# Layer 0 of a four-layer sequence kernel: row sums of squares from token-ordered sums, their scales through DRAM

## The chip, the cores and the metric

The kernel runs on one core of one Trainium2 chip. The metric is the device time of one execution in microseconds (us), given as the median of several executions. A profiled execution gives its own time, its span (first to last instruction) and the rows quoted below.

## The reference, cut to what matters

x is (64, 64, 256) in float32, which is 4096 tokens (rows) of D = 256. Four conditioned layers follow each other. The change touches the first one and the normalisation at the head of the second:

```python
def layer0(x, cond, norm_w, up_w, down_w):
    scale = cond @ norm_w.T + 1.0
    ms = jnp.mean(x * x, axis=-1, keepdims=True)
    h = x * (scale[:, None, :] * jax.lax.rsqrt(ms + EPS))
    val, gate = jnp.split(h @ up_w.T, 2, axis=-1)
    h = val * jax.nn.gelu(gate, approximate=False)
    y = act_quant(h) @ weight_quant(down_w).T
    return y + x

def layer1(x, t, ...):
    h = gamma1 * (x * rsqrt(mean(x * x, -1) + EPS)) + beta1   # then q, k, v
    x = x + alpha1 * (softmax(q k / 4) v @ W_o.T)
    h = gamma2 * (x * rsqrt(mean(x * x, -1) + EPS)) + beta2
    return x + alpha2 * ((silu(h @ gate_w.T) * (h @ hidden_w.T)) @ out_w.T)
```

Layer 2 is an adapter whose weights are made from cond, and layer 3 is a conditioned layer norm.

## The kernel before, in words

**Layout.** x stays in SBUF as `x_sb` with the 256 features on partitions (two halves of 128) and the tokens along the free axis. A number that belongs to a token, such as 1/rms, is then needed in every partition, in a row of 4096 columns: that row is `stat`. Layer 0's output y comes out of TensorE the other way round, tokens on partitions.

**Layer 0** goes over 32 tiles of 128 tokens as a software pipeline: one body per tile and engine, written in the order in which each engine executes it, and each helper works on an older tile (its lag). The order is fixed by hand; semaphores hold the engines together. For tile t, step by step:

- POOL `split_tile` makes the scaled input as a high and a low part, TensorE `up_chunk` projects it (24 matmuls of 512 columns per tile, L395), ACT takes the gelu (L503) and DVE multiplies (L620).
- DVE `largest` and `quantise` (L628, L576, L580) make 8-bit values, the SP queue transposes them by DMA (L271), and TensorE `down` multiplies them by the ternary weights (L412, 8 matmuls) into bank 4. It runs at the end of the body of tile t + 2.
- ACT `take_y` scales that to `y` (L494), TensorE `y_transposes` turns it (L431, 2 transposes), and DVE `add_y` adds it to `x_sb` (L569).
- For layer 1's normalisation ACT `square` squares the new x (L486), POOL `sum_squares` adds the two halves (L357), TensorE `row_squares` adds over partitions with a matrix of ones (L420), and DVE `take_row_squares` copies the row to `stat` (L592).

A plain copy of the tokens in token order (`tokens`, a ring of 4, L259) is read from DRAM for the input's own mean square (L478); ACT asks for it two tiles ahead.

**SP** issues, in each body: the transposing DMA, a piece of layer 1's weights (`w_stage`, L262), the tokens of one tile (L259).

**Between layer 0 and 1.** The last three or four tiles of layer 0 are finished inside the first attention tiles: the steps e32 to e36 are calls of layer 0's helpers put between attention's. `early_rstd` on ACT (in the body of tile 28) turns the first 768 columns of `stat` into 1/rms with two loads of activation tables around it (L515 to L520).

**Attention (layer 1)** has 16 tiles of 256 tokens, again one body per tile. ACT `attention_rstd` takes logarithm and exponential of the tile's 256 columns of `stat` (L168, L171). POOL `attention_input` multiplies x by them (L186) and applies gamma and beta (L190, L192) and makes the low part (L195). POOL also divides the softmax (`normalise`, L848) and adds the result to x (`residual`, L857). DVE takes the maxima and subtracts them (L1382, L1385), ACT exponentiates (L1192), DVE sums (L1395, L1399). The body of TensorE is squares (L1033), values (L970), scores (L991), transposes (L1005), output (L1045), keys (L940), weighted values (L1022), scores, transposes, queries (L940), transposes.

The lines that a sentence can't say well: who waits in the middle of the old chain.

```python
def row_squares(pe, s):
    if s.live(5):
        pe.wait_ge(Z["sq_sum_done"], s.at(5) + 1)
        wait(pe, Z["ss_done"], s.at(5))
        pe.wait_ge(Z["x_done"], s.at(3) if s.live(3) else N)
        nc.tensor.matmul(ss_ps, core["ones"][:], sq_sum[:, s.slot(5, 2), :], ...)
```

Of the kernel before, what the change touches and what calls it, by code (L numbers as in the profile page):

```python
# [104 lines left out]
def program(nc, io, out):  # L105
    with ExitStack() as ctx:
        def sb(name, shape, dt=FP32, c=ctx):
# [10 lines left out]
            ident_bf=sb("ident_bf", [P, P], BF16),  # L118
# [5 lines left out]
        with ExitStack() as c0:  # L124
# [10 lines left out]
                            "ln_done rstd_done xn_done h_done h_hi_done h_ready passed".split()}  # L135
        core["softmax"] = [sb(name, [P, 2, 8]) for name in ("mx", "rsum", "rec")]
        core["gen_cond"] = [sb(name, [P, B]) for name in ("gen_cond", "gen_factors")]

        adapter_w = nc.dram_tensor("adapter_w", [B, P * GEN_N], FP32, kind="Internal").ap()
# [24 lines left out]
def attention_rstd(nc, act, core, t):  # L164

    S = core["att_sems"]
    st = core["stat"][:, bass.ds(t * GT1, GT1)]
    nc.scalar.activation(st, st, ACT.Ln, scale=1.0 / D, bias=core["wscale"][:, 3:4]).then_inc(S["ln_done"], 1)  # L168
    act.wait_ge(S["ln_done"], t + 1)
    hold(act, S["passed"])  # L170
    nc.scalar.activation(st, st, ACT.Exp, scale=-0.5).then_inc(S["rstd_done"], 1)  # L171


def attention_input(nc, pool, core, t, k, part):

    x, cond, stat, h, S = core["x"], core["cond"], core["stat"], core["att_in"], core["att_sems"]
    hi, lo = (parts[k] for parts in core["att_parts"])
# [5 lines left out]
    if part == 0:  # L183
        pool.wait_ge(S["rstd_done"], t + 1)
# [20 lines left out]
def layer0(nc, io, core, bank, sb, sem, early):  # L205
# [11 lines left out]
    READY = 3 * GT1  # L217
# [18 lines left out]
    sq, sq_sum = sb("sq0", [P, 2, DH, P]), sb("sq0_sum", [P, 2, P])  # L236
    squared, ss, small, cond_t = sb("squared", [P, D]), sb("ss", [P, N]), sb("small", [P, 4, 4]), sb("cond_t", [C, B])
    y_ps, ss_ps, yt_ps = bank[4][:, 0:D], bank[7][:, 0:P], bank[7][:, P:P + DH * P].rearrange("p (h t) -> p h t", h=DH)
    norm_ps, down_ps, late_ps = bank[7][:, 0:DH * B], bank[7][:, 0:1], bank[7][:, DH * B:4 * DH * B]
    loaded_up, tokens_loaded, stage_loaded = ([sem(f"{n}{i}") for i in range(4)] for n in ("loaded_up", "tokens_loaded", "stage_loaded"))  # L240
    qt_loaded = [sem(f"qt_loaded{i}") for i in range(2)]
    names = ("loaded_norm loaded_cond loaded_vecs loaded_down loaded_x0 loaded_x1 loaded_x norm_ready norm_done cond_ready cond_done "
             "ones_done ident_done up_hi_done up_lo_done down_sum down_total down_step downq_done squared_done mean_done rstd0_done "
             "xs_done xs_hi_done xs_ready up_done gelu_done h_done small_step y_scale_done round_done q_done "
             "y_ready y_done yt_ready x_done sq_done sq_sum_done ss_ready ss_done w1_hi_done w1_lo_done passed sp_passed ve_passed").split()
    Z = {n: sem("z_" + n) for n in names}

    def sync_program(sp):
# [16 lines left out]
        def transpose_q(s):  # L265
            if s.live(3):
                k = s.slot(3, 2)
                sp.wait_ge(Z["q_done"], s.at(3) + 1)
                wait(sp, Z["y_ready"], s.at(5) + 1 if s.live(5) else 0)
                hold(sp, Z["sp_passed"])  # L270
                sp.dma_start_transpose(qt[:, k], q[:, k]).then_inc(qt_loaded[k], 16)  # L271

        def body(s):

            transpose_q(s)
            wait(sp, Z["w1_lo_done"], s.at(3))
            load_stage(s)
            sp.wait_ge(Z["squared_done"], s.at(3))
            load_tokens(s)

# [26 lines left out]
        pipeline(sp, N, 0, 4, body, start=4)  # L307
        for t in range(N, N + 3):
            transpose_q(Step(t, t % 4, N))
# [42 lines left out]
    def sum_squares(pool, s):  # L352
        if s.live(5):
            k = s.slot(5, 2)
            pool.wait_ge(Z["sq_done"], s.at(5) + 1)
            wait(pool, Z["ss_ready"], s.at(6))
            nc.gpsimd.tensor_tensor(sq_sum[:, k], sq[:, k, 0], sq[:, k, 1], ALU.add).then_inc(Z["sq_sum_done"], 1)  # L357

    def gpsimd_program(pool):
        def body(s):  # L360
# [6 lines left out]
            if s.last(-1):  # L367
                attention_input(nc, pool, core, 0, 0, 0)
                attention_input(nc, pool, core, 0, 0, 1)
            if s.last(0):  # L370
                attention_input(nc, pool, core, 0, 0, 2)
                attention_input(nc, pool, core, 1, 1, 0)
                attention_input(nc, pool, core, 1, 1, 1)
            sum_squares(pool, s)
# [3 lines left out]
        pipeline(pool, N, 5, 4, body, stop=N)  # L378
# [36 lines left out]
    def row_squares(pe, s):  # L415
        if s.live(5):
            pe.wait_ge(Z["sq_sum_done"], s.at(5) + 1)
            wait(pe, Z["ss_done"], s.at(5))
# [1358 lines left out]
```

## Time and profile before

| | |
|---|---|
| time, median of 3 runs | 814.53 us (813.87 to 815.04) |
| the profiled execution: its time / its span | 815.97 us / 813.9 us |
| TensorE (PE) busy | 783.1 us, 96% of the span |
| DVE, POOL, ACT busy | 541.9 us, 402.9 us, 375.8 us |
| granted TensorE clock, mean | 0.992 |
| layer 0 up to its last up projection | 0 to 233.3 us |
| attention | to about 425 us |
| the rest of layer 1, layers 2 and 3 | to 813.9 us |

"Busy" of TensorE counts modelled ends of pipelined matmuls, so neighbours overlap: what a group of matmuls costs is the distance to the start of the next one, which the chain of waits gives. An idle time in a timeline row stands in brackets, with what ended it.

### The profile page before, as it was taken

What the parts mean: (1) busy time and instruction counts of PE and PEld (TensorE: products, weight loads), DVE (VectorE), ACT (ScalarE), POOL (GpSimd) and SP (SyncE); (2) the same over time, 40 slices, a digit from 0 to 9 for tenths busy, and PEclk for the clock granted to TensorE, in tenths of its full rate; (3) what the DMA queues carried; (4) which work ended last, traced back from release to release, by engine and by line L of the source; (5) the groups of instructions that cost most, each with busy time, mean ns of one, the idle gap of its engine ahead of it and who ended that gap; (6) DMA issues with size and microseconds to landing.
All of it is one profiled execution on the core that took longest, in us unless ns stands there. A gap on an engine that the chain in (4) does not pass through costs nothing.

```text
span 813.9 us, 19536 instructions
## 1 busy us (share of the span) xinstructions
PE 783.1 (96%) x6860; PEld 630.4 (77%) x6860; DVE 541.9 (67%) x933; ACT 375.8 (46%) x729; POOL 402.9 (50%) x451
## 2 busy tenths in 40 slices
PE   8999999999999899999999999999999999999984
PEld 6788888888888898998988766676767677787772
DVE  4777777777789898898895555555454545444664
ACT  4244444444658688888875324322223222322332
POOL 3655555555596988888883531313131313101565
PEclk9999999999999999999999999999999999999997
DMA  8843333333320100000003087767667676592442
GB/s 248 234 79 78 77 77 77 77 77 78 77 41 7 38 3 1 0 0 0 0 2 104 22 262 234 233 180 223 194 201 205 183 208 193 181 374 98 156 167 104
DMA packets 73731, 97.57 MB, mean 120 GB/s; under 512 B 38608, under 2 KB 48016, under 8 KB 73552
## 3 DMA queue, kind: packets, MB, share of 16 engines
q1 hardware_dynamic: 71088, 92.68, 39.3%
q10 hardware_dynamic: 2592, 4.20, 1.4%
q8 instruction: 34, 0.56, 0.3%
q14 instruction: 17, 0.14, 0.1%
HBM read 67.23 MB, written 21.23 MB: 109 GB/s over the span
## 4 chain that ended last, share of the span: by engine, by line
PE 65%; POOL 16%; issue 8%; DVE 3%; DMA 3%; ACT 3%; SPq 1%; POOLq 1%; ACTq 0%; DVEq 0%
PE bank L1081 21%; PE bank L395 20%; PE bank L1095 11%; PE bank L1115 4%; POOL p_sb L848 4%; PE bank L412 3%; POOL mlp_in L186 2%; DMA early<-in_cond_w 2%; POOL mlp_in L190 2%; POOL x_sb L857 1%; POOL mlp_in L192 1%; POOL x_sb L1665 1%; POOL sums L1659 1%; POOL sums L1654 1%; POOL att_in_lo L195 1%
## 5 line engine op out<-in xcount | busy, mean ns | idle before, releaser
L1447 DVE TENSOR_TENSOR g<-bank,silu 128x512 f32<-128x512 f32 x64 | 44.2, 691 | 106.4 <-ACT silu L1292 56.6
L1292 ACT ACTIVATE silu<-bank 128x512 f32<-128x512 f32 x64 | 38.3, 598 | 111.3 <-PE bank L1081 111.3
L1298 ACT ACTIVATE g_hi<-g 128x512 fp32r<-128x512 f32 x64 | 40.4, 632 | 98.4 <-DVE g L1447 96.4
L395 PE MATMUL bank<-up_hi,xs_hi 128*128 128x512 f32 x256 | 83.0, 405 | 1.6 <-DVE h L620 0.8
L1450 DVE TENSOR_TENSOR g_lo<-g,g_hi 128x512 fp32r<-128x512 f32 x64 | 52.7, 824 | 45.3 <-ACT g_hi L1298 45.3
L395 PE MATMUL bank<-up_lo,xs_hi 128*128 128x512 f32 x256 | 80.6, 397 | 0.7 <-DVE up_lo L657 0.7
L1081 PE MATMUL bank<-mlp_in_hi,w_hi 128*128 128x512 f32 x256 | 80.6, 396 | 0.0
L848 POOL TENSOR_TENSOR p_sb<-p_sb,rec 128x512 f32<-128x512 f32 x64 | 66.7, 1046 | 27.6 <-DVE rec L1399 27.6
L1081 PE MATMUL bank<-mlp_in_lo,w_hi 128*128 128x512 f32 x256 | 79.8, 393 | 0.0
L1081 PE MATMUL bank<-mlp_in_hi,w_lo 128*128 128x512 f32 x256 | 79.7, 392 | 0.0
L395 PE MATMUL bank<-up_hi,xs_lo 128*128 128x512 f32 x256 | 79.4, 392 | 0.0
L620 DVE SCALAR_TENSOR_TENSOR h<-bank,rstd,gelu 128x512 f32<-128x512 f32 x64 | 47.8, 747 | 42.0 <-ACT gelu L503 42.0
L688 POOL TENSOR_TENSOR mlp_in_lo<-mlp_in,mlp_in_hi 128x1024 fp32r<-128x1024 f32 x8 | 22.7, 2836 | 97.9 <-ACT mlp_in_hi L695 97.9
L503 ACT ACTIVATE gelu<-bank,rstd 128x512 f32<-128x512 f32 x64 | 43.9, 687 | 56.2 <-PE bank L395 53.8
L678 POOL TENSOR_TENSOR mlp_in<-x_sb,stat 128x1024 f32<-128x1024 f32 (+1 forms) x8 | 19.1, 2387 | 78.8 <-PE bank L1081 78.6
L395 PEld LDWEIGHTS bank<-up_lo,xs_hi 128*128 128x128 f32 x256 | 48.3, 189 | 12.4 <-DVE up_lo L657 1.9
L395 PEld LDWEIGHTS bank<-up_hi,xs_lo 128*128 128x128 f32 x256 | 48.4, 189 | 11.0
L1081 PEld LDWEIGHTS bank<-mlp_in_lo,w_hi 128*128 128x128 f32 x256 | 48.1, 188 | 11.2
L1081 PEld LDWEIGHTS bank<-mlp_in_hi,w_hi 128*128 128x128 f32 x256 | 47.9, 188 | 11.3 <-issue 0.2
L1081 PEld LDWEIGHTS bank<-mlp_in_hi,w_lo 128*128 128x128 f32 x256 | 48.1, 188 | 11.0
L395 PEld LDWEIGHTS bank<-up_hi,xs_hi 128*128 128x128 f32 x256 | 45.7, 190 | 11.4 <-POOL xs_lo L332 2.0
L1095 PE MATMUL bank<-g_hi,w_hi 128*128 128x512 f32 x128 | 54.2, 423 | 0.0
(193 smaller groups left out, 1916.3 us busy)
## 6 DMA issues: line engine op xcount, KB each, us to landing
gen_hyper<-in_gen_t SPq DMA_DIRECT2D x32, 512.0 KB, 4.9
gen_made<-base_w SPq DMA_DIRECT2D x64, 256.0 KB, 3.9
adapter_w<-gen_made SPq DMA_DIRECT2D x64, 256.0 KB, 3.5
tokens<-in_x_tok SPq DMA_DIRECT2D x32, 128.0 KB, 2.3
w_stage<-in_w_t SPq DMA_DIRECT2D x32, 128.0 KB, 2.4
weight_slot<-adapter_w SPq DMA_DIRECT2D x4, 1024.0 KB, 9.0
w_hi<-adapter_w SPq DMA_DIRECT2D x4, 1024.0 KB, 5.7
w_lo<-adapter_w SPq DMA_DIRECT2D x4, 1024.0 KB, 9.4
```

The source lines that it names most:

```text
L395: last = nc.tensor.matmul(bank[2 * j + part][:, :], (xs_hi, xs_lo)[a][:, k, d, :], up[b][:, d, at:at + 512], start=n == d == 0, stop=n == ...
L412: last = nc.tensor.matmul(y_ps, qt[:, s.slot(2, 2), f, :], downq[:, f, :], start=f == 0, stop=f == FC - 1)
L503: nc.scalar.activation(gelu[:, j, :], bank[2 * j + 1][:, :], ACT.Gelu, scale=rstd0[:, bass.ds(s.at(0), 1)]).then_inc(Z["gelu_done"], 1)
L620: nc.vector.scalar_tensor_tensor(out=h[:, k, j * 512:(j + 1) * 512], in0=bank[2 * j][:, :], scalar=rstd0[:, bass.ds(t, 1)], in1=gelu[:, j, ...
L848: nc.gpsimd.tensor_tensor(pu, pu, rec[:, r % 2, :].unsqueeze(2).to_broadcast([P, 8, L]), ALU.mult).then_inc(A["norm_done"], 1)
L1081: last = nc.tensor.matmul(bank[2 * (f % 2) + i][:, :], w1[a][:, at:at + P], hs[b][k][:, d, :], start=n == d == 0, stop=n == 2 and d == DH - 1)
L1095: last = nc.tensor.matmul(bank[5 + m][:, :], w1[a][:, at:at + P], gs[b][:, f % 2, :], start=f == n == 0, stop=f == FC - 1 and n == 2)
L1115: last = nc.tensor.matmul(ps[B * half:B * (half + 1), :], scaled[rows, :], hyper[rows, k, half, :], start=True, stop=True)
L1292: nc.scalar.activation(silu[:, f % 2, :], bank[2 * (f % 2)][:, :], ACT.Silu).then_inc(S["silu_done"], 1)
L1298: nc.scalar.activation(gs[0][:, f % 2, :], g[:, f % 2, :], ACT.Copy).then_inc(S["g_hi_done"], 1)
L1447: nc.vector.tensor_tensor(g[:, f % 2, :], bank[2 * (f % 2) + 1][:, :], silu[:, f % 2, :], ALU.mult).then_inc(S["g_done"], 1)
L1450: nc.vector.tensor_tensor(gs[1][:, f % 2, :], g[:, f % 2, :], gs[0][:, f % 2, :].bitcast(FP32), ALU.subtract).then_inc(S["g_ready"], 1)
```

## The change

In layer 0, what was in feature order becomes token order:

- A second copy of the tile's tokens (`tokens_again`, a ring of 2) is read from DRAM. DVE `add_tokens` makes y = scale * (down result) + tokens in one operation; `take_y` and `add_y` go.
- TensorE transposes this sum, and ACT `take_x` copies the transposed result over the tile of `x_sb`, where x was.
- ACT `square_rows` squares y with its accumulator, so that a tile's sums of squares lie in one column of `row_squares` (128 x 32). `square`, `sum_squares`, `row_squares` (PE) and `take_row_squares` go.
- For each group of 4 tiles POOL `row_scales` adds EPS and raises to -0.5 (128 x 4). SP stores these 512 numbers to DRAM in token order, and in the next body reads them back, spread over all partitions, into 512 columns of `stat`. `early_rstd` and `attention_rstd` go; `attention_input` waits for the loaded columns instead.
- The bf16 identity, which nothing read, goes.

```diff
+    def add_tokens(ve, s):
+        if s.live(3):
+            t, k = s.at(3), s.slot(3, 2)
+            ve.wait_ge(Z["y_ready"], t + 1)
+            ve.wait_ge(Z["y_scale_done"], t + 1)
+            ve.wait_ge(again_loaded[k], 16 * s.turn(3, 2))
+            wait(ve, Z["yt_ready"], t)
+            wait(ve, Z["rows_done"], t)
+            nc.vector.scalar_tensor_tensor(out=y[:], in0=y_ps, scalar=small[:, s.slot(3, 4), 3:4], in1=again[:, k, :],
+                                           op0=ALU.mult, op1=ALU.add).then_inc(Z["y_done"], 1)
...
+    def square_rows(act, s):
+        if s.live(3):
+            t = s.at(3)
+            act.wait_ge(Z["y_done"], t + 1)
+            wait(act, Z["rows_done"], t)
+            nc.scalar.activation(squared_rows[:], y[:], ACT.Square, scale=D ** -0.5,
+                                 accum_out=row_squares[:, bass.ds(t, 1)]).then_inc(Z["rows_done"], 1)
...
+    def take_x(act, s):
         if s.live(4):
+            act.wait_ge(Z["yt_ready"], s.at(4) + 1)
+            nc.scalar.activation(x[:, :, bass.ds(s.at(4) * P, P)], yt_ps, ACT.Copy).then_inc(Z["x_done"], 1)
...
+    def row_scales(pool, s):
+        if s.slot(0, 4) == 3 and s.live(7):
+            group = bass.ds(s.at(7), 4)
+            pool.wait_ge(Z["rows_done"], s.at(7) + 4)
+            nc.gpsimd.tensor_tensor(row_squares[:, group], row_squares[:, group], wscale[:, 3:4].to_broadcast([P, 4]),
+                                    ALU.add).then_inc(Z["row_mean_done"], 1)
+            pool.wait_ge(Z["row_mean_done"], s.turn(7, 4))
+            nc.gpsimd.tensor_tensor(row_rstd[:, group], row_squares[:, group], wscale[:, 5:6].to_broadcast([P, 4]),
+                                    ALU.pow).then_inc(Z["row_rstd_done"], 1)
...
     # SP, after the transposing DMA, the weights and the tokens of each body:
+        def load_again(s):
+            if s.live(3):
+                wait(sp, Z["y_done"], s.at(4) if s.live(5) else 0)
+                sp.dma_start(again[:, k, :], io["x_tok"][:, bass.ds(s.at(3) * D, D)]).then_inc(again_loaded[k], 16)
+        def store_rows(s):
+            if s.slot(0, 4) == 2 and s.live(10):
+                sp.wait_ge(Z["row_rstd_done"], s.turn(10, 4))
+                sp.dma_start(rstd_row[bass.ds(s.at(10) * P, 4 * P)].rearrange("(t p) -> p t", p=P),
+                             row_rstd[:, bass.ds(s.at(10), 4)], allow_slow_non_contiguous=True).then_inc(Z["row_stored"], 16)
+        def spread_rows(s):
+            if s.slot(0, 4) == 3 and s.live(11):
+                sp.wait_ge(Z["row_stored"], 16 * s.turn(11, 4))
+                wait(sp, stat_loaded, 16 * s.turn(11, 4) - 16)
+                sp.dma_start(stat[:, bass.ds(s.at(11) * P, 4 * P)],
+                             rstd_row[bass.ds(s.at(11) * P, 4 * P)].unsqueeze(0).to_broadcast([P, 4 * P])).then_inc(stat_loaded, 16)
...
     # attention_input, part 0
-        pool.wait_ge(S["rstd_done"], t + 1)
+        pool.wait_ge(core["stat_loaded"], 16 * s.turn(0, 2))
...
     # layer 0's last steps inside attention: DVE
-            first["add_y"](ve, e32)
+            first["add_tokens"](ve, e32)
             ve.wait_ge(A["v_cleared"], 1)
             take_values(a2)
-            first["take_row_squares"](ve, e32)
-            first["add_y"](ve, e33)
+            first["add_tokens"](ve, e33)
             maxima(a2, 0)
             maxima(a2, 1)
-            first["take_row_squares"](ve, e33)
-            first["add_y"](ve, e34)
             sums(a2, 0)
             sums(a2, 1)
+            first["add_tokens"](ve, e34)
             maxima(a2, 2)
             maxima(a2, 3)
```

How the instructions stand now, at the places of which the prediction speaks. First DVE, from the end of layer 0's last body (L628 to L632 before are `largest` of tile 31) to the first softmax maxima. Before:

```order
L592 COPY stat<-bank 128x128
L576 TENSOR_SCALAR h<-h,small 128x1024
L580 TENSOR_SCALAR q<-h 128x1024
L585 TENSOR_SCALAR small<-small,wscale 128x1
L569 TENSOR_TENSOR x_sb<-x_sb,bank 128x2x128
L1411 COPY v_sb<-bank 64x2x8x16
L1412 COPY v_sb<-bank 64x2x8x16
L592 COPY stat<-bank 128x128
L569 TENSOR_TENSOR x_sb<-x_sb,bank 128x2x128
L1382 TENSOR_REDUCE mx<-bank 128x8
```

And with the change (L587 is `add_tokens`, L595 and L599 the quantisation):

```order
L595 TENSOR_SCALAR h<-h,small 128x1024
L599 TENSOR_SCALAR q<-h 128x1024
L604 TENSOR_SCALAR small<-small,wscale 128x1
L587 SCALAR_TENSOR_TENSOR y<-bank,small,tokens_again 128x256
L1404 COPY v_sb<-bank 64x2x8x16
L1405 COPY v_sb<-bank 64x2x8x16
L587 SCALAR_TENSOR_TENSOR y<-bank,small,tokens_again 128x256
L1375 TENSOR_REDUCE mx<-bank 128x8
```

The two copies to `stat` are gone, and what stands behind the quantisation is now the operation whose result TensorE transposes. Further down, the third `add_tokens` (tile 31) stands before the maxima of units 2 and 3:

```order
L1388 TENSOR_REDUCE rsum<-p_sb 128x8
L1392 RECIPROCAL rec<-rsum 128x8
L587 SCALAR_TENSOR_TENSOR y<-bank,small,tokens_again 128x256
L1375 TENSOR_REDUCE mx<-bank 128x8
L1378 TENSOR_TENSOR p_sb<-bank,mx 128x512
```

Before, nothing of layer 0 stood between those sums and maxima (its `add_y` for that tile came two attention steps later).

## Rows read from the trace of the kernel before

**Rows 1.** Busy time by stretch: us, PE, PEld, DVE, ACT, POOL, clock, DMA share, GB/s.

```profile
60.00:220.00 160.00, 160.00 (x848) 134.68 (x847) 118.21 (x234) 70.34 (x168) 85.22 (x162) 1.00 0.34 76
302.90:326.90 24.00, 23.95 (x395) 21.62 (x394) 21.38 (x41) 20.21 (x41) 19.86 (x19) 1.00 0.01 2
```

**Rows 2.** Chain of waits, one tile of layer 0 (start us, us, what).

```profile
151.39 0.22 PE bank L420 x2
151.61 0.22 PE bank L431 x2
151.83 0.87 PE bank L412 x8
152.70 5.49 PE bank L395 x24
```

**Rows 3.** Chain of waits, the up projections of tiles 30 and 31.

```profile
220.78 5.72 PE bank L395 x24
227.82 5.51 PE bank L395 x24
```

**Rows 4.** Timeline of the body of tile 19 (start us, us, engine, what, idle before).

```profile
148.08 0.29 DVE L592 COPY stat<-bank 128x128 f32 x1 [0.18 <-issue]
148.17 0.42 ACT L478 ACTIVATE squared<-tokens 128x256 f32<-128x256 f32 x1 [2.39 <-DMA tokens<-in_x_tok]
148.29 0.41 DVE L569 TENSOR_TENSOR x_sb<-x_sb,bank 128x256 f32 x1
148.94 0.68 ACT L503 ACTIVATE gelu<-bank,rstd 128x512 f32<-128x512 f32 x1
150.16 0.74 DVE L620 SCALAR_TENSOR_TENSOR h<-bank,rstd,gelu 128x512 f32<-128x512 f32 x1
```

**Rows 5.** DMA issues from 60 to 220 us (count, KB, us to landing).

```profile
DMA packets 31334, 12.20 MB, mean 76 GB/s; under 512 B 25444, under 2 KB 31332, under 8 KB 31332
tokens<-in_x_tok SPq DMA_DIRECT2D x23, 128.0 KB, 2.3
qt<-q SPq DMA_TRANSPOSE x24, 3.1
```

**Rows 6.** Timeline of POOL behind the early scales on ACT.

```profile
218.48 0.74 POOL L349 TENSOR_TENSOR w_lo<-w_stage,w_hi 128x256 fp32r<-128x256 f32 x1 [3.75 <-ACT w_hi L509]
```

**Rows 7.** Timelines of PE and DVE between layer 0 and attention.

```profile
234.34 0.49 PE L420 MATMUL bank<-sq_sum,ones 128*128 128x128 f32 x2 [1.02 <-POOL sq_sum L357]
240.56 0.46 PE L420 MATMUL bank<-sq_sum,ones 128*128 128x128 f32 x2 [0.34 <-DVE x_sb L569]
...
248.00 0.66 DVE L1382 TENSOR_REDUCE mx<-bank 128x8 f32<-128x512 f32 x1
...
248.51 1.05 PE L412 MATMUL bank<-downq,qt 128*128 128x256 bf16 x8
...
262.57 0.29 DVE L592 COPY stat<-bank 128x128 f32<-128x128 f32 x1 [0.76 <-PE bank L420]
```

**Rows 8.** Chain of waits, steady attention: what releases POOL's next input.

```profile
350.24 0.42 ACT stat L171
```

**Rows 9.** Timelines of all engines, one attention tile in its steady part.

```profile
337.58 0.49 ACT L168 ACTIVATE stat<-stat,wscale  x1
337.85 0.43 DVE L1411 COPY v_sb<-bank 64x256 f32<-64x256 f32 x1
340.30 0.63 ACT L1192 ACTIVATE p_sb<-p_sb 128x512 f32<-128x512 f32 x1 [0.42 <-DVE p_sb L1385]
343.19 1.04 POOL L848 TENSOR_TENSOR p_sb<-p_sb,rec 128x512 f32<-128x512 f32 x1 [0.53 <-DVE rec L1399]
345.69 0.63 ACT L1263 ACTIVATE sq<-x_sb 128x512 f32 x1 [0.67 <-POOL x_sb L857]
347.87 0.30 PEld L970 LDWEIGHTS bank<-w_hi,att_in_hi 128*128 128x128 f32 x2 [0.22 <-ACT q_sb L1250]
349.81 0.43 DVE L1411 COPY v_sb<-bank 64x256 f32<-64x256 f32 x1
```

More of the change, by code:

```diff
@@ L161, with attention_input @@
 V_OUTB, V_BD, V_BU, V_LNW, V_LNB, V_LINB, V_EVEN, V_ODD = 0, 2, 3, 5, 7, 9, 11, 12
[L164 to L174, printed above, removed]
+def attention_input(nc, pool, core, s, part):
     x, cond, stat, h, S = core["x"], core["cond"], core["stat"], core["att_in"], core["att_sems"]
-    hi, lo = (parts[k] for parts in core["att_parts"])
+    t = s.at(0)
+    hi, lo = (parts[s.slot(0, 2)] for parts in core["att_parts"])
     hb = h[:].rearrange("p h (b l) -> p h b l", b=GB1)
@@ L306, in sync_program @@
                 transpose_q(Step(3, 3, N))
-        pipeline(sp, N, 0, 4, body, start=4)
-        for t in range(N, N + 3):
-            transpose_q(Step(t, t % 4, N))
+                load_again(Step(3, 3, N))
+        pipeline(sp, N, 11, 4, body, start=4, stop=N)
+        for t in range(N, N + 8):
+            s = Step(t, t % 4, N)
+            transpose_q(s)
+            load_again(s)
+            store_rows(s)
+            spread_rows(s)
     def split_tile(pool, s):
@@ L413, in down @@
             last.then_inc(Z["y_ready"], 1)
[L415 to L418, printed above, removed]
-            pe.wait_ge(Z["x_done"], s.at(3) if s.live(3) else N)
-            nc.tensor.matmul(ss_ps, core["ones"][:], sq_sum[:, s.slot(5, 2), :], start=True, stop=True).then_inc(Z["ss_ready"], 1)
     def y_transposes(pe, s):
@@ L634, in body @@
         def body(s):
-            add_y(ve, s)
+            add_tokens(ve, s)
             quantise(ve, s)
@@ L1130, in _ @@
             values(a2)
-            first["row_squares"](pe, e32)
             first["y_transposes"](pe, e32)
@@ L1135, in _ @@
             keys(a2)
-            first["row_squares"](pe, e33)
             first["y_transposes"](pe, e33)
@@ L1142, in _ @@
             transposes(a2, 1)
-            first["row_squares"](pe, e34)
             first["y_transposes"](pe, e34)
@@ L1317, in _ @@
             take_values(a2)
-            first["square"](act, e32)
             nc.scalar.preload_act_table_set("natural_log_exp_and_others")
-            first["take_y"](act, e33)
+            first["take_x"](act, e33)
             act.wait_ge(A["v_ready"], 1)
@@ L1324, in _ @@
             exponentials(a2, 1)
-            first["square"](act, e33)
+            first["square_rows"](act, e33)
             take_keys(a2)
@@ L1328, in _ @@
             take_queries(a2)
-            first["take_y"](act, e34)
+            first["take_x"](act, e34)
             exponentials(a2, 3)
-            first["square"](act, e34)
+            first["square_rows"](act, e34)
             take_transposed(a2, 0)
```

151 lines of the change are left out of this document (52 added, 99 removed).

## The prediction, made before the changed kernel ran

> **What bounds the kernel now.** I read the busy time by stretch first. In layer 0's loop TensorE is busy for all of 160 us, the clock at its full level (1.00, that is 2.4 GHz), while DVE has 118 us, POOL 85 and ACT 70 [rows 1]. So a tile costs what TensorE executes in it. The chain of waits says what that is: 0.22 us for `row_squares` (L420), 0.22 for the transposes, 0.87 for `down`, 5.49 for the up projections, together 6.80 us, one piece directly behind the other [rows 2]. In a steady attention tile TensorE is nearly full too (23.95 of 24.00 us for two tiles), but DVE, ACT and POOL have 21.4, 20.2 and 19.9 us, and 12 us per tile may just as well be the length of a circle through all of them [rows 1]. Between the two stages TensorE stands still several times [rows 7]. After attention nothing is changed.
>
> **The sum is made against the profiled execution (815.97 us)**, which is 1.44 us above the median shown.
>
> **1. Layer 0's loop on TensorE.** `row_squares` runs in the bodies of tiles 5 to 31. In 26 of them (5 to 30) it lies before the last up projection, each 0.22 us on the bounding engine [rows 2]: 26 x 0.22 = **-5.7 us**. Nothing is added on TensorE. Whether the other engines keep up with 6.58 us per tile is the question of the next points.
>
> **2. DVE in the loop.** Before: L592 (starts 148.08) and L569 (148.29, 0.41 us) stand in front of the quantisation [rows 4]. Now it is one `add_tokens`, also one PSUM operand and one SBUF operand of 256 columns, so I take L569's 0.41 us; the 0.21 us of L592 go. It waits for more than `add_y` did, for `down`. But `down` of the tile ends at 145.9 (151.83 + 0.87 = 152.70 is the same point one body later, minus 6.80 [rows 2]), and DVE only gets there at 148.1 [rows 4]: 2.2 us in hand. Cost 0.
>
> **3. ACT in the loop.** One copy replaces another, and the square is now taken with an accumulator, as L478 is. L478, its reading and `take_y` together take 0.77 us (148.17 to 148.94 [rows 4]), so the square becomes at most 0.36 us longer, between the two gelus, where ACT has idle time: the gelu of the first half starts at 148.94, and its product (L620) is over at 150.90, 1.8 us before TensorE needs the bank at 152.70 [rows 2, 4]. What ACT waits for is its token load, 2.39 us in this body [rows 4]. Cost 0, the cover is this 1.8 us.
>
> **4. POOL.** 0.5 us of `sum_squares` per tile goes from an engine with half its time free; two tiny operations per four tiles come. Cost 0 in the loop.
>
> **5. The DMAs.** `tokens_again` is one more load like `tokens` (2.3 us to landing [rows 5]), about 8 us of bodies before DVE wants it: it is requested behind the quantised tile's transposing DMA two bodies earlier, so there is more than one body (6.6 us) against 2.3 us. The queues move 76 GB/s at a share of 0.34 [rows 1]; this adds 128 KB per 6.6 us, 20 GB/s. The store of 512 numbers of 4 bytes has no equal in the trace. Lower bound: nothing, it is issued behind all that the body needs, and 4 us of quiet follow until the next transposing DMA. Upper bound, by the nearest row: a transposing DMA is 25,444 / 24 = 1,060 packets below 512 B and lands after 3.1 us [rows 5], so 512 pieces should take less than that. I take 0. The read back is asked for a body later and each group is needed long before, except the last one, for attention tile 14. SP's own waits (for y two tiles back, for POOL's scale, for the store) are all over when it gets to them. The Trainium skill, "DMA: Bandwidth & Descriptors" (Specifications; Rules for kernel authors), speaks against this store: a non-contiguous last dimension becomes one descriptor per element, and below 512 B the engine does a read-modify-write. [...]
>
> **6. The early scales on ACT.** Two table loads, a logarithm and an exponential go. They held POOL for 3.75 us [rows 6], and one body later TensorE shows a hole: the chain has 5.72 us instead of 5.49 in the body of tile 30 [rows 3]. **-0.23 us.** No other hole is to be seen there.
>
> **7. Between the layers.** Call E the end of the last up projection, 227.82 + 5.51 = 233.33 [rows 3]. Behind it TensorE waited 1.02 us for `sum_squares`. This stop goes, but the time isn't won: the next stop (0.34 us, ended by DVE's L569 at 240.5) hangs on DVE, which from E on does product, maximum, quantisation, scale, addition. Now the transposes of tile 29 wait for `add_tokens` at the same place of that row, so this stop grows by what the first one loses. What really leaves is L592 ahead (0.21) and L420 itself (0.22): **0.4 us** ahead of before. Then comes a new wait: `add_tokens` of tile 31 stands before the maxima of units 2 and 3 and needs `down` of tile 31. Before, these maxima started at 248.00, ahead of that `down` (248.51, 0.87 us long) [rows 7]. Now they start behind `down` and an addition: 248.51 + 0.87 + 0.41 - 0.4 = 249.4 + about 0.1 for the semaphores, 1.3 to 1.5 us late, and with them exponentials 2 and 3 and all queued behind them. Against this stand, in the next body, three L592 and one L569 that leave DVE, L420 twice, and the stop of 0.76 us in front of the last L592 [rows 7], together some 2.1 us on DVE's row. Net I take **-0.5 us** for the stage. Bounds: the delay stays whole and only 0.5 us comes back, +0.9; or nothing is late and all comes back, -2.1.
>
> **8. Steady attention.** `attention_rstd` goes: two operations of 0.49 us and less per tile on ACT. The chain of waits passes through it in every second tile [rows 8], which would promise up to 0.9 us per pass. I count 0, because the circle that has to close every 12 us doesn't contain it: DVE's copy of the values at 337.85, maxima, sums, then POOL's division (343.19, which had waited 0.53 for DVE), the addition to x, ACT's square (345.69, had waited 0.67 for POOL), the queries, TensorE's weight load (347.87, had waited 0.22 for ACT's queries), DVE's next copy at 349.81, 11.96 us later [rows 9]. L168 (337.58) lies where ACT afterwards waits 0.42 us for DVE anyway [rows 9]. It just waits longer.
>
> Sum: -5.7 - 0.23 - 0.5 = **-6.4 us**: 809.6 for the profiled execution, **808.1** for the median.
>
> **The rivals.**
> - **A, attention gets faster.** If ACT's part closes the circle after all, each of about 11 steady tiles wins up to the 0.22 us by which TensorE waits for ACT's queries [rows 9]: -2.4 us more, 805.7. For it: the chain goes through L171 [rows 8]; against it: the 0.42 us of slack behind it. 0.15.
> - **B, the new order is paid in full.** DVE's wait for the last `down` is handed on into the POOL-heavy tiles and isn't made good: +0.9 instead of -0.5, 809.5. 0.15.
> - **C, slower: the store clogs the queues.** If 512 pieces keep the DMA engines so long that the next tile's tokens come late, ACT holds both gelus, and TensorE stops in 7 of the 32 bodies. From where: tokens are issued 0.9 us before the store and again 6.6 us later; they may land 2 us later than now before L620 misses TensorE. So it begins when a store takes more than about 5.7 + 2 = 7.7 us, and to undo 6.4 us and lose the 1.6 us that could be measured, each must cost 8/7 = 1.1 us more: 8.8 us per store. At 10 us the loss is 16 us less 6.4, 824.1. The 3.1 us for twice the number of pieces [rows 5] speaks against it; 4-byte writes to DRAM are what no row shows. 0.05.
> - **D, it is not the ones-matmul that filled the gap**: the transposes, now directly behind an up projection, take over its weight-load time and only half of the 0.22 us is won, 2.9 us less: 811.0. The rows show no idle time between pieces, so I give it 0.05.
>
> **The numbers.** The forecast (808.1, its own range 807 to 809) has 0.6. The range, 804.5 to 811, takes in A, B and D and the bounds of point 7, and leaves out C. A measurement of this kernel can tell about 0.2%, 1.6 us, from no change; A, B, D and the forecast are all faster by more. Faster 0.92, same 0.03, slower 0.05.
>
> **What would show it.** Right: the chain's up projections in layer 0 follow each other at 6.58 us; the body of tile 30 has no hole; behind E one stop of about 1.5 us in front of the transposes of tile 29, ended by `add_tokens`; a wait of about 1.5 to 2 us in front of the third `add_tokens`; attention tiles still 12.0 us apart, with ACT's wait for DVE in front of the exponentials grown by nearly 1 us. Wrong: TensorE idle in every fourth body (C), transposes or `down` longer in the chain (D), attention tiles 11.8 us apart (A), or a waiting `add_tokens` in the loop itself, which would refute point 2.

## The result, and the profile after

**835.34 us** median (832.72 to 836.58, 4 runs) against 814.78 for the kernel before beside it (813.87 to 816.31): ratio **1.0246**, 95% interval 1.0217 to 1.0276. The change makes the kernel 2.5% slower; the forecast was 808.1 us. The profiled execution took 834.95 us, with a span of 833.2.

I cut each profile at two marks: the last start of a matmul of the group `up_hi,xs_hi`, shortly before layer 0's up projections end (L395 before, L429 after), and the start of the first MLP matmul (L1081, L1079). All in us; the first column is from the program's start.

| kernel | layer 0's last | first MLP | span | between the marks | from MLP to the end |
|---|---|---|---|---|---|
| before | 232.0 | 428.3 | 813.9 | 196.3 | 385.6 |
| the change | 236.2 | 441.5 | 833.2 | 205.3 | 391.7 |

So 19.3 us of span came in three places: 4.2 in layer 0, where 5.9 should have been won; 9.0 between the marks; 6.1 behind them, where nothing was changed.

Busy time by stretch of the changed kernel (us, PE, PEld, DVE, ACT, POOL, clock, DMA share, GB/s), to be read beside [rows 1]:

```profile
60.00:220.00 160.00, 151.34 (x773) 123.29 (x772) 114.75 (x204) 63.90 (x182) 91.10 (x151) 1.00 0.47 103
302.90:326.90 24.00, 23.89 (x400) 21.59 (x396) 21.43 (x41) 18.65 (x36) 19.90 (x18) 1.00 0.01 2
260.00:300.00 40.00, 33.06 (x518) 30.18 (x517) 26.77 (x51) 23.40 (x45) 28.76 (x27) 0.87 0.13 29
785.00:833.00 48.00, 31.42 (x510) 24.56 (x506) 24.93 (x44) 14.28 (x26) 28.06 (x29) 0.81 0.34 122
```

TensorE, busy all the time in layer 0 before, now stands still for 8.7 of 160 us. Steady attention is what it was. Behind layer 0 and at the end the granted clock is down.

**Layer 0.** The chain of waits through one of the stops:

```profile
164.26 1.25 SPq L267
165.70 0.43 SPq L257
166.23 5.97 DMA tokens<-in_x_tok
172.45 0.07 ACT squared L502
173.39 0.70 ACT gelu L528
174.21 0.76 DVE h L632
175.01 1.19 PE bank L429 x4
```

The tokens take 5.97 us instead of 2.3 [rows 5], ACT holds its gelus for them, and TensorE waits for the bank. The chain has such a wait at 108.94, 137.73, 166.23, 195.20 and 223.65, in every fourth body. What SP had issued ahead (its timeline):

```profile
160.52 0.41 SPq L281 DMA_DIRECT2D rstd_row<-row_rstd  x1
166.23 0.39 SPq L254 DMA_DIRECT2D tokens<-in_x_tok  x1
170.64 0.35 SPq L290 DMA_DIRECT2D stat<-rstd_row  x1
```

L281 is the store of 512 numbers, L290 waits until it is complete: 10.1 us. The waits on SP's queue add them up (queue, line, released by: us, times, longest), and the DMA page shows how little the engines do:

```profile
SPq L102 <- DMA rstd_row<-row_rstd: 35.3, 8, 9.7
```

```profile
DMA packets 38009, 16.41 MB, mean 103 GB/s; under 512 B 28534, under 2 KB 37366, under 8 KB 38006
tokens<-in_x_tok SPq DMA_DIRECT2D x23, 128.0 KB, 2.7
rstd_row<-row_rstd SPq DMA_DIRECT2D x6, 2.0 KB
```

Share 0.47, median of the tokens still 2.7: a mean hides a stop that comes in one body of four.

**Between the layers.** Timeline and chain of waits:

```profile
244.30 0.44 PE L456 MATMUL bank<-ident,y 128*128 128x128 f32 x2 [1.41 <-DVE y L587]
253.10 0.48 DVE L587 SCALAR_TENSOR_TENSOR y<-bank,small,tokens_again 128x256 f32<-128x256 f32 x1 [2.04 <-PE bank L446]
...
270.73 0.69 DVE L1375 TENSOR_REDUCE mx<-bank 128x8 f32<-128x512 f32 x1 [6.98 <-remote]
270.83 0.60 ACT L1196 ACTIVATE pt_sb<-bank 128x512 f32<-128x512 f32 x1 [4.14 <-remote]
```

```profile
263.58 7.17 another core or an unknown queue
```

The first two rows are the two waits that the forecast named. The other three are new: DVE and ACT stand still together and go on at 270.7. SP goes on at 270.87, released by the last store (issued at 260.63). The profile names no releaser ("remote"), but the semaphores are the program's own. DVE waits for the one that TensorE's scores count up, ACT for the one of TensorE's transposes:

```profile
263.03 1.10 PE L993 MATMUL bank<-k_sb,q_sb 32*64 32x128 f32 x32
268.97 0.27 PE L1007 MATMUL bank<-ident,p_sb 128*128 128x128 f32 x1 [0.50 <-issue]
```

The scores end at 264.13 by the profile, and the trace records their two signals at 270.70 and 270.75; the transposes' first is recorded at 270.80. Meanwhile TensorE goes on starting matmuls, until 268.97. So what comes 6.6 us late is TensorE's signals. (Some other semaphore records of this stretch are missing in the trace, so of the other engines it says less.) Two queues that bring instructions move one transfer each in that stretch, at 263.1 and 266.6. TensorE stands from 269.24 to 273.34 and has a clock of 0.60 in the 10 us from 270 on.

**The ending.** A wait of TensorE that the kernel before has nowhere in its ending (line, released by: us, times, longest):

```profile
PE bank L1591 <- issue: 3.1, 1, 3.1
```

From 791.9 on TensorE stops in the middle of a row of matmuls, waiting for nothing that the profile shows; the clock is 0.50 to 0.54 in the 6 us from 794 on.

### The profile page after: what moved, and what is told of

The parts are those of the page before. It is cut to its first block, busy times and chain, and to the rows that moved or that the text cites. A ratio compares the mean times of both kernels' runs of the same rounds, so it can differ in the third digit from the quotient of the medians.

```text
span 833.2 us, 19402 instructions
## 1 busy us (share of the span) xinstructions
PE 782.3 (94%) x6796; PEld 626.7 (75%) x6796; DVE 540.5 (65%) x900; ACT 360.6 (43%) x731; POOL 408.7 (49%) x435
## 4 chain that ended last, share of the span: by engine, by line
PE 53%; POOL 15%; issue 10%; DMA 8%; DVE 7%; SPq 3%; ACT 2%; another core or an unknown queue 1%; POOLq 1%; DVEq 0%; ACTq 0%
PE bank L1079 20%; PE bank L1093 11%; PE bank L429 10%; DMA tokens<-in_x_tok 4%; POOL p_sb L855 4%; PE bank L1113 4%; POOL mlp_in L179 2%; POOL mlp_in L183 2%; DMA early<-in_cond_w 1%; POOL mlp_in L185 1%; PE bank L1602 1%; POOL x_sb L864 1%; PE bank L1614 1%; DVE h L632 1%; PE bank L446 1%
## 5 line engine op out<-in xcount | busy, mean ns | idle before, releaser
L429 PE MATMUL bank<-up_hi,xs_hi 128*128 128x512 f32 x256 | 82.2, 402 | 3.3 <-POOL xs_lo L360 1.6
L1079 PE MATMUL bank<-mlp_in_hi,w_hi 128*128 128x512 f32 x256 | 80.6, 396 | 0.0
L1079 PE MATMUL bank<-mlp_in_lo,w_hi 128*128 128x512 f32 x256 | 79.8, 393 | 0.0
L632 DVE SCALAR_TENSOR_TENSOR h<-bank,rstd,gelu 128x512 f32<-128x512 f32 x64 | 47.9, 748 | 49.1 <-ACT gelu L528 48.5
L1079 PE MATMUL bank<-mlp_in_hi,w_lo 128*128 128x512 f32 x256 | 79.7, 392 | 0.0
L429 PE MATMUL bank<-up_lo,xs_hi 128*128 128x512 f32 x256 | 79.4, 391 | 0.0
L429 PE MATMUL bank<-up_hi,xs_lo 128*128 128x512 f32 x256 | 79.1, 390 | 0.0
L1375 DVE TENSOR_REDUCE mx<-bank 128x8 f32<-128x512 f32 x64 | 43.9, 686 | 19.4 <-PE bank L993 11.9
L1079 PEld LDWEIGHTS bank<-mlp_in_lo,w_hi 128*128 128x128 f32 x256 | 48.1, 188 | 11.2
L1079 PEld LDWEIGHTS bank<-mlp_in_hi,w_hi 128*128 128x128 f32 x256 | 47.9, 188 | 11.3 <-issue 0.2
L1079 PEld LDWEIGHTS bank<-mlp_in_hi,w_lo 128*128 128x128 f32 x256 | 48.1, 188 | 11.1
L429 PEld LDWEIGHTS bank<-up_lo,xs_hi 128*128 128x128 f32 x256 | 47.9, 188 | 11.1 <-DVE up_lo L665 0.9
L429 PEld LDWEIGHTS bank<-up_hi,xs_hi 128*128 128x128 f32 x256 | 45.5, 188 | 14.0 <-DVE h L632 2.7
L429 PEld LDWEIGHTS bank<-up_hi,xs_lo 128*128 128x128 f32 x256 | 48.1, 188 | 10.4
## 6 DMA issues: line engine op xcount, KB each, us to landing
weight_slot<-adapter_w SPq DMA_DIRECT2D x4, 1024.0 KB, 10.1
```

The costliest lines, as they stand in the source:

```text
L429: last = nc.tensor.matmul(bank[2 * j + part][:, :], (xs_hi, xs_lo)[a][:, k, d, :], up[b][:, d, at:at + 512], start=n == d == 0, stop=n == ...
L632: nc.vector.scalar_tensor_tensor(out=h[:, k, j * 512:(j + 1) * 512], in0=bank[2 * j][:, :], scalar=rstd0[:, bass.ds(t, 1)], in1=gelu[:, j, ...
L1079: last = nc.tensor.matmul(bank[2 * (f % 2) + i][:, :], w1[a][:, at:at + P], hs[b][k][:, d, :], start=n == d == 0, stop=n == 2 and d == DH - 1)
L1375: nc.vector.tensor_reduce(mx[:, r % 2, :], sc, AX.X, ALU.max).then_inc(A["max_done"], 1)
```

## The experiments

Theory T: a store in 4-byte pieces takes 8 to 10 us until it is signalled, and whatever is issued behind it, tokens, weights, instructions, is signalled only after it. R1: it is the second token copy. R2: any small store to DRAM costs this. T's part on instructions was my reading of the stop behind layer 0; no run shows it, and experiment 5 speaks against it.

**1. Wider pieces.**

```
-  rstd_row[...].rearrange("(t p) -> p t", p=P)    # 512 pieces of 4 bytes
+  rstd_row[...].rearrange("(p t) -> p t", p=P)    # 128 pieces of 16 bytes
   (attention_input reads stat[:, group].rearrange("p (q f) -> p f q", f=4))
```

> The same 2 KB per store, but written as 128 pieces of 16 bytes instead of 512 of 4, and POOL reads the scales in the order in which they then stand; everything else, the second copy of the tokens included, as in the change. Theory T (a store of 512 pieces takes 9.7 us until its completion is signalled, and every DMA issued behind it, tokens, weights, the program's own instructions, is signalled only after it): with a quarter of the pieces, between a token load's 2.4 us and 9.7 us, about 2.4 + 7.3/4 = 4.2 us per store, below the 7.7 us at which TensorE begins to feel it; layer 0 ends near 227 us, the 7 us stop near 264 us is gone, in all 806 to 811 us. Rival R1 (it is the second token copy, its load or the longer row of SP's waits): stays at 833 to 837 us. Rival R2 (any store of this kind to DRAM costs the 9.7 us, whatever its pieces): stays there too, with the store still at 9 to 10 us.

813.31 us (809.44 to 816.05), ratio to before 0.9991 (0.9975 to 1.0008). The store takes 1.6 us (247.6 to 249.2, where SP waits for nothing else), no stop in layer 0, none between the marks. R1 and R2 fall: the second copy is still there, and so is a store of 2 KB. The median is 2 us above the expectation; the profiled execution (809.44) has a clock of 0.994, the slowest (816.05) 0.984.

**2. The scales turned on TensorE.**

```
+  nc.tensor.transpose(bank[5][0:4, 0:P], row_rstd[:, 0:4], ident)
+  nc.scalar.activation(row_t, bank[5][0:4, 0:P], ACT.Copy)
-  store of row_rstd[:, 4 columns] as 512 pieces of 4 bytes
+  store of row_t as 4 pieces of 512 bytes, two bodies later
```

> The four columns of scales are turned by one small transpose on TensorE per four tiles, ACT copies the result, and the store is 4 pieces of 512 bytes; it is issued two bodies later. Theory T: the store takes about as long as a token load, 2 to 3 us, no stop in layer 0 and none near 264 us: 807 to 811 us, against 814.8 before and 835.3 for the change. R1: stays near 835 us. R2: store still 9 to 10 us, time near 835 us.

809.47 us (808.08 to 811.01), ratio **0.9936** (0.9919 to 0.9954). Its window and its last store with the read back behind it:

```profile
60.00:220.00 160.00, 160.00 (x836) 133.02 (x836) 122.54 (x218) 70.22 (x201) 99.21 (x160) 1.00 0.45 109
```

```profile
256.91 0.29 SPq L282 DMA_DIRECT2D rstd_row<-row_t  x1
258.25 0.36 SPq L291 DMA_DIRECT2D stat<-rstd_row  x1
```

Store 1.3 us, TensorE full again. This is the change without its fault, and it wins most of what was forecast.

**3. The stores alone, in the kernel before.**

```
+  eight stores of 512 x 4 bytes from a constant tile, at the change's places in SP's row
```

> The kernel before, unchanged, plus the eight stores of 512 numbers of 4 bytes at the same places of SP's row as in the change, from a tile that is set once; nobody waits for them and nothing reads them, so the output is unchanged. No second token copy, no read back. Theory T: every fourth body loses 2 to 2.6 us, some 8 to 10 us in layer 0, where before loses nothing, and a stop of several us comes soon after layer 0 when instructions are fetched behind the last store: 826 to 834 us. R1: 814 to 816 us, as before. R2: as T.

819.49 us, ratio 1.0058 (1.004 to 1.0077): slower as T says, by 5 us and not by 12 to 19. The tokens behind a store take 4.75 to 6.00 us here too. Four bodies take 28.05 us (120.16 to 232.36 over 16) against 27.23: 0.8 us per store, where the change loses 2.2 (28.56, from 117.53 to 231.76 over 16, against 26.39 in x2_turned). Part of it is seen: the next tokens are issued 6.3 us behind the store here (162.43, 168.73) and 5.7 in the change, and the bodies are 0.22 us longer. The rest I can't account for. And there is no stop behind layer 0 (196.9 us between the marks), against the forecast. The last store goes out at 246.8, hardly earlier than the one that brings a stop in experiment 10 (247.41), and an instruction transfer follows it at 248.6; why it holds nothing up stays open.

**4. Only the last two stores wider.**

```
+  rows = rows.rearrange("(p t) -> p t", p=P) if after the loop else rows.rearrange("(t p) -> p t", p=P)
```

> The change with only its last two stores (those after the loop) written as 128 pieces of 16 bytes; the scales of tiles 24 to 31 come out in another order of tokens, nothing else is changed. It separates layer 0 from what follows. Theory T: layer 0 ends at 237.5 us as in the change (at 235 to 237.5, since the last but one store lies near its end), the stop of 7.2 us near 264 us is gone together with most of the low clock behind it: 9 us off, 824 to 828 us, and down to 820 us if the low clock at the end of the program was a consequence. If the stop near 264 us has nothing to do with the last store: 833 to 837 us.

831.26 us (829.89 to 832.85): 4 us off, not 9. Between the marks 197.6 us: the 7.2 us stop is gone, as T says, and the clock is 1.00 from 270 us on (0.83 in the 10 us before). But layer 0 ended at 242.4 instead of 236.2, with a clock below 1 in several places, and the ending stayed at 391.1 us: no consequence of that stop alone.

**5. The stores by themselves**, on SP while it is idle in attention.

```
+  for each shape: sp.dma_start(shape).then_inc(s, 16); sp.wait_ge(s, ...)
```

> The stores by themselves: the kernel before, in which SP, idle during attention, issues one DMA after another and waits for each. The output is unchanged, nothing reads what they store. In this order: stores of 512, 256, 128 and 1024 pieces of 4 bytes; stores of 128 pieces of 16, 8 and 32 bytes; a load of 128 KB like the tokens'; the 512-piece store with such a load right behind it; the 128 pieces of 16 bytes with a load right behind; a load with the 512-piece store right behind it; last a read of 512 pieces of 4 bytes. Theory T: 9.7 us for 512 pieces, 1.6 us for 128 pieces of 16 bytes, about 2.3 us for the load alone, but over 9 us for the load that stands behind the 512 pieces, near 2.5 us for the one behind the 16-byte pieces, and 2.3 us for the load that stands in front. If the price is per piece: about 5.5, 3.5 and 18 us for 256, 128 and 1024 pieces. If it is the 4-byte width and not the number: 128 pieces of 4 bytes near 9 us as well. Rival to T: the load behind the store takes 2.3 us too, then the stops in layer 0 have another cause.

Timeline of SP; a DMA's time is the distance to the next row, since SP waits in between (not between rows 0.4 us apart, issued as a pair). In order: 512, 256, 128, 1024 pieces of 4 bytes (L823); 128 of 16, 8, 32 bytes (L827); a load; 4-byte store and load; 16-byte store and load.

```profile
279.94 0.39 SPq L823 DMA_DIRECT2D lab_row<-rstd  x1
288.15 0.37 SPq L823 DMA_DIRECT2D lab_row<-rstd  x1
297.41 0.33 SPq L823 DMA_DIRECT2D lab_row<-rstd  x1
305.04 0.36 SPq L823 DMA_DIRECT2D lab_row<-rstd  x1
315.84 0.33 SPq L827 DMA_DIRECT2D lab_row<-rstd  x1
318.29 0.33 SPq L827 DMA_DIRECT2D lab_row<-rstd  x1
321.10 0.32 SPq L827 DMA_DIRECT2D lab_row<-rstd  x1
322.50 0.33 SPq L830 DMA_DIRECT2D lab_in<-in_x_tok  x1
324.62 0.37 SPq L823 DMA_DIRECT2D lab_row<-rstd  x1
325.03 0.51 SPq L830 DMA_DIRECT2D lab_in<-in_x_tok  x1
333.20 0.32 SPq L827 DMA_DIRECT2D lab_row<-rstd  x1
```

512 pieces 8.2 us, 256 9.3, **128 still 7.6**, 1024 10.8; 16, 8, 32 bytes wide 2.4, 2.8, 1.4. The load: 2.1 alone, **8.2 behind the 4-byte store**, 4.7 behind the 16-byte one (333.56 to 338.24, more than I expected). The busy share of the DMA engines, 40 slices of the first store's 8.2 us:

```profile
DMA  0000370000000000000000020000000000000000
```

The pieces are moved in slices 5 and 6, about 1.2 us after the issue; then 7 us of silence until the signal (the 2 is an instruction transfer). So a busy share can't show this cost.

The run itself took 831.81 us (one execution; the kernel before beside it 813.28). Two stops like the change's lie in its attention:

```profile
309.77 5.44 another core or an unknown queue
326.97 6.56 another core or an unknown queue
```

The first ends at 315.2, about when the store of 1024 pieces is signalled (SP goes on at 315.84), the second at 333.5, as the 512 pieces with the load are (333.20). Again TensorE's score signals are what comes late, by 4.7 and 5.8 us; and in the second stop no queue moves instructions (none from 316 to 340 us; the whole run has 34 and 17 transfers on the two queues, as before has, so none is missing). So a held fetch of instructions isn't what this stop waits for. The other four 4-byte stores of the run bring no stop, so one more condition is missing.

**6. The widths.**

```
+  store(lab_row[0:16].rearrange("(p t) -> p t", t=1), 16, 1)    # 16 pieces of 4 bytes; the others alike
```

> Again the kernel before with DMAs one at a time on the idle SP during attention: stores of 1, 16 and 128 pieces of 4 bytes, of 128 pieces of 8 and of 12 bytes, of 512 pieces of 8 bytes; reads of 128 pieces of 4, 8 and 16 bytes; a store of 128 pieces of 8 bytes with a load of 128 KB behind it; the store of 128 pieces of 4 bytes with a load behind it; a load; a read of 512 pieces of 4 bytes; a load. If it is the width of 4 bytes that costs, whatever the number: 7 to 9 us for 128 pieces of 4 bytes, probably for 16 too, and 2.5 to 3.5 us for 512 pieces of 8 bytes and 12-byte pieces. If the number matters as well: under 4 us for 1 and 16 pieces, over 4 us for 512 of 8 bytes. Reads: 2 to 3 us all, if only the write to DRAM is slow; 7 to 9 us for 4-byte reads, if the width alone decides. The load behind 4-byte pieces 7 to 9 us, behind 8-byte pieces below 5.

Read in the same way: 1, 16, 128 pieces of 4 bytes 1.1, 3.0, 7.6 us; 128 of 8 bytes 4.5, of 12 bytes 3.5; **512 of 8 bytes 3.25**. Reads of 128 pieces of 4, 8, 16 bytes 3.7, 1.7, 2.5, and of 512 scattered 4-byte pieces 2.1. A load behind the 8-byte store 5.1, behind 128 4-byte pieces 7.9 (with a stop of 4.3 us in attention). Each is one measurement, and 128 pieces of 8 bytes took 2.8 us in experiment 5, so differences of 2 us say little. Neither simple rule holds: for 4-byte pieces written to DRAM the number counts up to about 128 and hardly beyond, and 512 pieces of 8 bytes are no dearer than 128. The run took 818.03 us (one execution, before beside it 816.22).

**7. The store on ACT's queue.**

```
-  sp.dma_start(rstd_row[...], row_rstd[...])
+  nc.scalar.dma_start(rstd_row[...], row_rstd[...])    # behind square_tokens, every fourth body
```

> The change with its store of 512 pieces of 4 bytes issued by ACT, on its own DMA queue, at about the same time as before by SP; the read back is asked for one body later. Theory T in the form that one queue works in order: tokens on SP's queue land in 2.4 us again, layer 0 ends near 227 us, the stop near 264 us is gone unless instructions share that queue: 808 to 813 us, plus up to 1 us for the eight issues on ACT. Theory T in the form that the 16 engines signal in order whatever the queue: tokens still land after 5 to 6 us in every fourth body, 831 to 837 us.

855.75 us, ratio 1.0514 (1.0477 to 1.0552), worse than the change and above both forecasts. A stop (timelines of SP and ACT):

```profile
174.40 0.39 ACTq L516 DMA_DIRECT2D rstd_row<-row_rstd  x1
178.46 0.38 SPq L254 DMA_DIRECT2D tokens<-in_x_tok  x1
186.00 0.35 SPq L282 DMA_DIRECT2D stat<-rstd_row  x1
186.84 0.42 ACT L492 ACTIVATE squared<-tokens 128x256 f32<-128x256 f32 x1 [8.48 <-DMA tokens<-in_x_tok]
```

The store is on another queue, and the tokens on SP's still wait for it: the hold passes across queues. Here the store takes up to 11.6 us and the tokens are asked for 4 us behind it, hence the longer stops. The Trainium skill, "DMA: Bandwidth & Descriptors" (Queues, rings and completion order), says that a semaphore's increment lands only after every earlier write of the same DMA engine, across its queues. Experiments 5 and 7 agree; by that rule the forecast would have had to put the store's full time in front of the next tokens.

**8. A stop without stores**, in the kernel before.

```
+  SP: ten loads of 128 KB, one behind the other; PE waits for the last before attention's loop
```

> The kernel before with nothing of the change: TensorE alone is held at the start of attention's loop until ten small loads, one behind another, have landed, a stop of some 8 to 14 us from about 252 us on, of the kind that the change has at 264 us. If a stop of that length lets TensorE's granted clock fall behind it and moves the rest of the program so that its ending meets a low clock too, the time grows by the stop plus 4 to 8 us, and the mean clock of the runs is 0.975 to 0.985 as in the change. If a stop costs its own length only: the time grows by just that, with a clock of 0.992.

831.37 us (827.16 to 833.37), ratio 1.0209; clocks 0.980 to 0.984. TensorE stood from 249.0 to 261.0, and its clock was 0.50 from 256 to 270. From the MLP to the end it took 387.7 us, with such a wait in its ending:

```profile
PE bank L1613 <- issue: 2.6, 1, 2.6
```

At the first MLP matmul this profile is 13.7 us behind before, at its end 15.8: the ending costs 2.1 us more without any store in the program (the medians, of other executions, differ by 18.1). But a late arrival alone doesn't do it. Experiment 5's profile reaches the MLP at 444.1, 15.8 us late, and takes 385.7 us from there with no such wait; x1_pieces16 reaches it early, at 420.9, and has one of 2.0 us. All six profiles of the change and of the versions that don't turn the scales have a wait of 1.8 to 3.4 us there, the four of the turned version none; of the variants of the kernel before, this one and x10_widths (2.3 us) have it, x3_before_store and x5_alone don't. So it goes with the program rather than with the time of arrival.

**9. The third addition behind the maxima.**

```
-  add_tokens(e34); maxima(a2, 2); maxima(a2, 3)
+  maxima(a2, 2); maxima(a2, 3); add_tokens(e34)
```

> The version with the turned store, and the third addition of tokens between the layers put behind the maxima of units 2 and 3 instead of ahead of them. If that new wait is what makes the stretch from layer 0's end to the MLP's first tile 1.5 us longer than before (196.5 us against 195.0): 1 to 2 us faster than the turned version, 807.5 to 808.5 us. If the stretch is bound otherwise (transposes that wait for ACT's copies of x, or the additions themselves): no change, 809 to 810 us, or slower, since the last transposes of layer 0 come later.

808.53 us, ratio 0.9944 (0.9921 to 0.9967), by the runs no better than the turned version. By the traces the stretch between the marks goes from 197.8 to 195.6 us. Ahead the turned version, then this one:

```profile
241.05 0.48 DVE L609 SCALAR_TENSOR_TENSOR y<-bank,small,tokens_again 128x256 f32<-128x256 f32 x1 [2.05 <-PE bank L449]
244.43 0.41 PE L459 MATMUL bank<-ident,y 128*128 128x128 f32 x2 [2.54 <-ACT x_sb L531]
```

```profile
241.13 0.48 DVE L609 SCALAR_TENSOR_TENSOR y<-bank,small,tokens_again 128x256 f32<-128x256 f32 x1
241.67 0.44 PE L459 MATMUL bank<-ident,y 128*128 128x128 f32 x2 [0.16 <-DVE y L609]
```

The addition waits 2.05 us for `down`; the maxima, ACT's exponentials and ACT's copy of x queue behind it, and the transposes wait 2.54 us for that copy. I ran both again side by side, with the 16-byte version in the same order:

> The version with the turned store once more, beside the two that follow on the same chip. 808 to 811 us.

> The same with the third addition behind the maxima, once more beside it. In the two profiles TensorE's first MLP matmul came 2.2 us sooner after layer 0's last one; if that is a property of the order, this version is 1 to 2 us faster than the turned one here too; if it is eaten by the ending, the two are within 1 us.

> The version with 128 pieces of 16 bytes, which needs neither the small transpose nor ACT's copy, with the third addition behind the maxima: layer 0 as there, the stretch between the layers 1 to 2 us shorter, 807 to 812 us, where the spread is the ending's: x1_pieces16 ran from 809.4 us at a clock of 0.994 to 816.1 at 0.984.

811.67 (ratio 0.9946), **809.09 (0.9919, 0.9898 to 0.994)** and 812.32 us (0.9945). Now the order is worth 2.6 us in the medians and 2.2 between the marks (197.7 and 195.5), though the intervals overlap. The 16-byte version stays 3 us behind, its clock at 0.986 to 0.992; its profile has a wait of 1.8 us in the ending, and 390.8 us from the MLP to the end. The best version beats the kernel before by 0.6 to 0.8%.

**10. All but the last two stores wider.**

```
+  rows = rows.rearrange("(t p) -> p t", p=P) if after the loop else rows.rearrange("(p t) -> p t", p=P)
```

> The reverse of x4_last_two: the first six stores are 128 pieces of 16 bytes, only the two after the loop keep their 512 pieces of 4 bytes; the scales of tiles 0 to 23 come out in another order of tokens, nothing else is changed. Theory T: layer 0 ends at 225 to 227 us as in x1_pieces16 (the seventh store is issued near its end), the last store still holds the next fetch of instructions: a stop of 5 to 7 us soon after it with a low clock behind, the stretch from layer 0's last matmul to the MLP's first 7 to 9 us longer than the 197.9 us of x1_pieces16, and the ending, which comes some 8 us later than there, with or without its own stop: 818 to 826 us. If the stop near 264 us came from the delays of layer 0 and not from the last store: that stretch stays at 198 us, 810 to 815 us.

819.2 us, ratio 1.005 (1.003 to 1.007). Layer 0 is whole (last matmul at 223.1), the last store (4-byte) is issued at 247.41, and:

```profile
251.88 5.48 another core or an unknown queue
```

```profile
257.03 0.34 SPq L293 DMA_DIRECT2D stat<-rstd_row  x1
```

The stop ends at 257.36, as the store is signalled; from 250 to 258 us the DMA page has two packets, both of them instructions. Between the marks 203.7 us against x1_pieces16's 197.9, behind them 389.6 against 386.7, with a stop of 3.13 us in the ending (776.67). DVE waits for TensorE's score signals here too (recorded 4.9 us late). So the last store costs 5.8 us by itself. The ending is dearer too, but x1_pieces16 has a stop of 2.0 us in its own, so that isn't shown to be the store's doing.

## Why the prediction was wrong

**Points 1 and 6, right.** From the first steady up projection to the last (28 bodies) before takes 190.75 us (37.07 to 227.82), x2_turned 184.84 (34.98 to 219.82): -5.91, forecast -5.93. D did not happen, and the covers of points 2 to 4 held: TensorE full for 160 us. Not priced: in that version the first steady body starts 2.1 us sooner. About half of it is the profile of before, whose clock is 0.83 from 20 to 30 us (x3_before_store, with all of its work, starts there at 36.02); the rest I did not trace.

**Point 5, the step that failed.** "Upper bound, by the nearest row: a transposing DMA is ... 1,060 packets below 512 B and lands after 3.1 us". That row was near in the number of pieces and far in their kind: it writes to SBUF, and the price lies in 4-byte writes to DRAM, 7.6 us for as few as 128. The range ended at 3.1 us although no row showed such a write, as rival C says itself. "SP's own waits (...) are all over when it gets to them" fell with it (35.3 us of waits for the stores). The store's term in the sum was 0. It measured 2.2 us per store in layer 0, 12.2 us at layer 0's last up projections (236.2 against x2_turned's 224.0), and 7.5 us more between the marks.

**Rival C, right in its mechanism.** It put the threshold at 7.7 us, hence 2.4 us per store of 10.1; measured 2.2. It had no term for the last store, behind which TensorE's signals come late: 5.8 us alone (experiment 10) and 7.5 in the change (205.3 against x2_turned's 197.8), nor for the ending (391.7 against 386.2). So its 824.1 fell 11 us short, and 0.05 was far too little for the only case whose price had no row.

**Point 7, wrong beyond its bounds.** -0.5 forecast, +0.9 the upper bound, +1.5 measured (196.3 to 197.8 in x2_turned). The new wait was named and was real (2.04 us at DVE); I let the work that leaves DVE pay for it and did not follow it on to ACT's copy of x and the transposes (2.54 us). With the order turned round the stretch is 0.7 us shorter than before (195.6).

**Point 8, right.** DVE's copy of the values comes at 339.00 and 351.04:

```profile
339.00 0.43 DVE L1404 COPY v_sb<-bank 64x256 f32<-64x256 f32 x1
351.04 0.43 DVE L1404 COPY v_sb<-bank 64x256 f32<-64x256 f32 x1
```

12.04 us, with ACT's two operations gone. A is false.

**Open:** why x3_before_store loses only 0.8 us per store; why TensorE's signals come late beside some of the 4-byte stores and not beside others; and what makes the ending dearer. In the four profiles with a stop of about 3 us there (the change, x4_last_two, x11_all_but_two, x7_other_queue) the part behind the MLP takes 389.6 to 391.7 us; in the others it takes 384.7 to 387.8, except x9c_pieces16_maxima with 390.8. In the change the stop falls in a row of matmuls while the adapter's 2 MB of weights are under way (issued at 785.55, landing after 10.7 us); that the next instructions wait behind them is argued, not shown.

## What to carry to other kernels

Price a store by the width of its pieces before their number: a turn on TensorE and 512-byte pieces, or at least 8 or 16 bytes side by side, took 1 to 5 us where 128 or more 4-byte pieces to DRAM took 8 to 11. A DMA is not free because nobody waits for it: ask what is issued behind it, on every queue, and whether that is needed before the DMA is signalled. A wait to which the profile gives no releaser is not yet explained: look up whose semaphore it is. And where no row of the trace shows an operation of that kind, the range has to hold its bad case, or the operation is measured alone first.

## What the runs showed of the hardware

- Stores to DRAM in 4-byte pieces: 1.1, 3.0, 7.6, 9.3, 8.2 and 10.8 us for 1, 16, 128, 256, 512 and 1024 pieces; 512 pieces of 8 bytes 3.25 us. In the one looked at closely (512) the data has moved after 1.3 us, and the signal comes 7 us later.
- A load of 128 KB issued behind such a store is signalled with it, 8.2 us instead of 2.1, on the same queue and on another (tokens 8.1 us, from 178.46).
- Beside some such stores TensorE's score signals are recorded late, until about when the store is signalled: 6.6 us in the change, 4.9 in x11_all_but_two, 4.7 and 5.8 in x5_alone, 3.5 in x10_widths. DVE and ACT stand still for them.
- After a stop of 12 us the granted clock is at its lower level (0.50, 1.2 GHz) for 9 us of work (261 to 270) and then back (0.99 from 270 to 272); after the 4.1 us stop at 269 in the change it is low as well. Stops of 3 us in the ending have the same effect.
